# Matmuls without a result at sixteen PE steps of the first two and last two batches of a two-layer cross-attention kernel

## The chip, the cores and the metric

The kernel runs on one core of one Trainium2 chip. The metric is device time in microseconds of one execution. Three runs of the kernel before took 2371.49, 2372.46 and 2372.55 us; the median is 2372.46 us.

## The reference

For each of 64 batches there are 256 positions of 320 channels and a context of 77 tokens of 512 channels. Two cross-attention layers follow each other, each with 20 heads of 16 channels. Layer 0 and layer 1, cut to what is computed:

```python
# layer 0, all tensors per batch and head
q = x @ Wq.T; k = text @ Wk.T; v = text @ Wv.T          # text: the 77 tokens
out = softmax(q @ k.T * D**-0.5) @ v
x = (merge_heads(out) @ Wo.T + bo) + x
# layer 1
text, ip = ctx[:, :-4], ctx[:, -4:]                     # 73 text tokens, 4 image tokens
probs = softmax(q @ k_t.T * D**-0.5)
text_out = probs @ v_t
qsem = l2norm(probs @ text); sem = qsem @ l2norm(ip).T
probs_ip = softmax(q @ k_ip.T * D**-0.5 + 0.5 * sem) * spatial_mask
x = ((text_out + probs_ip @ v_ip) @ W_out + b_out) + x
```

## The kernel before

A first stage (to about 317 us) projects all contexts to keys and values and stores them in HBM. The second stage, `attention`, starts at about 321 us and goes through the 64 batches as a software pipeline. Each step of the pipeline has a name: the layer (0 or 1), a letter and a number. On PE, `q` is the query projection, `s` the scores whose maxima are wanted, `m` the turning of the maxima, `t` the turned scores (of which `0t0`, `0t1`, `0t2` fill PSUM for five exponentials), `a` the product of exponentials and values, `o` the output projection, and in layer 1 `u` and `n` the weighted squares of the semantic part, `i` and `p` the scores and values of the image tokens. ACT takes the exponentials (`ef`), DVE the maxima (`mneg`), the low halves (`q_low`) and the softmax of the image tokens (step `y`, 19 small operations, the last of which writes `pip`), POOL scales by the inverse sums (`ust`) and writes the low half of the attended values (`al`). Inverse sums go through HBM (`rb<-r_dram`), as do the image probabilities (`pt<-p_dram`).

The order on every engine is written out by hand: the table `ORDER` gives a cycle of steps, each with a lag in batches (`0o0/1` is the output projection of layer 0, one batch behind). At the beginning and at the end of the pipeline only the steps whose batch exists stand in the cycle, so PE has fewer of them between two waits. A batch is numbered from 0 to 63.

PSUM has 8 banks. The table `USES` says which steps use which bank, and `Turns` works out who used a bank last. Each PE step begins with `wait_free(...)`, which waits until the last reader of its banks is done, and then waits for its data with `b.reached(...)`:

```python
def turned_scores(l, b, c):
    ...
    wait_free(pe, l, b, *uses)
    if c == 0:
        b.reached(pe, s_ql[l], 2, 1)
        b.reached(pe, s_tw[l], 2, 2)
        b.reached(pe, s_mt[l], 1, 1)
```

For `0t1` the banks' last reader is the exponential of the step before (`0t0`), and there is no wait for data behind it. For the first `0o0` the bank is new and the only wait is for `al`. For the last `1p0` the banks' last readers include step `y` of the same batch, that is `pip`; its data wait is for `pt`, which is `pip` after its way through HBM.

PE's engine runs its instructions in this order, one after the other.

Of the kernel before, what the change touches and what calls it, by code (L numbers as in the profile page):

```python
# [16 lines left out]
B, S, C = 64, 256, 320  # L17
# [80 lines left out]
class Batch:  # L98
# [23 lines left out]
    def reached(self, eng, sem, each, k):  # L122
# [20 lines left out]
        0x/0 1sh/4 1rl/4 1ps/4 1sl/3 0k/0 0ds/1 1v/2 1pl/4 1c/1 0rw/1 0sh/1 0rl/1 1ds/3 1g/1 1ns/3 1d/3 0v/0 1nl/3  # L143
        1rw/3 1vi/2 1st/4 1ss/2 1k/1""",
}

FIRST = {}

# [595 lines left out]
def attention(nc, psum, early, x, k_dram, v_dram, g_dram, c_dram, kip_dram, vip_dram, r_dram, n_dram, s_dram, p_dram,  # L744
# [3 lines left out]
    with ExitStack() as stack:  # L748
# [12 lines left out]
        ident16, sel, pick, kmask, vmask = early.ident16, early.sel, early.pick, early.kmask, early.vmask  # L761
# [66 lines left out]
        def banks(l, use, n=1):  # L828
            r = min(turn_banks.banks(l, use))
            return psum[:, r:r + n, :]  # L830

        def row(l, use, n=1):
            return banks(l, use, n).rearrange("p r n -> p (r n)")
# [4 lines left out]
        def wait_free(eng, l, b, *uses, only=None):  # L838
            turn_banks.wait(eng, freed, b, l, *uses, only=only)

        def keys(l, both_parts, c):

            lead = both_parts * 4 * T + c * 2 * T if c < 2 else 8 * T + both_parts * 2 * T
            return ke[l][:, lead:lead + 2 * T].rearrange("p (e t) -> p e t", e=2)
# [5 lines left out]
        def in_halves(ap, j):  # L850

            return ap.rearrange("p h s -> p (h s)").rearrange("p (z h s) -> p z h s", z=2, s=TS)[:, :, j, :]
# [147 lines left out]
        def _(pe):  # L1000
            def project(o, w, tail, high, low, chunks, packed):

                for at_chunk, c in enumerate(chunks):
                    halves = packed and c == 2
                    cols = slice(c * P, c * P + (HALF if halves else P))
                    parts = [(w[:, hw, k, cols], high, k) for k in (0, 1) for hw in (0, 1)]
                    parts += [(tail[:, cols], high, 2)]
                    parts += [(w[:, 0, k, cols], low, k) for k in (0, 1)]
                    parts += [(tail[:, cols], low, 2)]
                    for n, (a, data, k) in enumerate(parts):  # L1010
                        at_ends = {"start": n == 0, "stop": n == len(parts) - 1}
                        if not halves:
                            mm = pe.matmul(o[:, at_chunk * S:(at_chunk + 1) * S], a, data[:, k, :], **at_ends)  # L1013
                            continue
                        for z in (0, 1):
                            mm = pe.matmul(o[z * HALF:(z + 1) * HALF, 0:TS], a, data[:, k, z * TS:(z + 1) * TS], **at_ends)  # L1016
                return mm

            def query(l, b, n):
                wait_free(pe, l, b, f"q{n}")  # L1020
                b.reached(pe, s_xh[l], 1, 1)
                b.reached(pe, s_xl[l], 1, 1)
                project(row(l, f"q{n}"), wqs[l], wqt[l], xh[l], xl[l], PARTS[n], True).then_inc(f_q[l], 1)

            def scores(l, b, c):

                n = TXT[l]
                uses = [f"s{2 * c}", f"s{2 * c + 1}"]
                wait_free(pe, l, b, *uses)
                if c == 0:  # L1030
                    b.reached(pe, s_qh[l], 2, 1)
                    b.reached(pe, s_ke[l], 16, 16)
                for s in range(2):
                    for j in range(NJ):
                        rows = slice(j * SLOT, (j + 1) * SLOT)
                        o = banks(l, uses[j // 2], 2)[:, j % 2, 0:4 * n].rearrange("p (e s t) -> p e s t", e=2, s=2)
                        mm = pe.matmul(o[:, :, s, :], qh[l][rows, c * S + s * P:c * S + (s + 1) * P],  # L1037
                                       keys(l, 0, c)[rows, :, 0:n], start=True, stop=True)
                if c == 1:
                    b.reached(pe, s_qh[l], 2, 2)  # L1040
                    for j in range(NJ):
                        rows = slice(j * SLOT, (j + 1) * SLOT)
                        o = banks(l, uses[j // 2], 2)[:, j % 2, 4 * n:6 * n].rearrange("p (e t) -> p e t", e=2)
                        mm = pe.matmul(o, qh[l][rows, 2 * S:PW], keys(l, 0, 2)[rows, :, 0:n], start=True, stop=True)
                mm.then_inc(f_s[l], 1)

            def turn_max(l, b, n):
                wait_free(pe, l, b, "m")
                b.reached(pe, s_max[l], MAXIMA, MAXIMA)
                o = row(l, "m").bitcast(F16)  # L1050
                for s in range(2):
                    mm = pe.transpose(o[:, s * P:(s + 1) * P], mneg[l][:, :, :, s].rearrange("p j x -> p (j x)"),  # L1052
                                      ident16[:])
                mm.then_inc(f_m[l], 1)

            def turned_scores(l, b, c):

                n = TXT[l]
                uses = [f"t{2 * c}", f"t{2 * c + 1}"] if c < 2 else ["t4"]
                wait_free(pe, l, b, *uses)  # L1060
                if c == 0:
                    b.reached(pe, s_ql[l], 2, 1)
                    b.reached(pe, s_tw[l], 2, 2)
                    b.reached(pe, s_mt[l], 1, 1)
                if c == 2:
                    b.reached(pe, s_ql[l], 2, 2)
                for e in range(2):
                    if c < 2:
                        tiles = [(slice(j * SLOT, (j + 1) * SLOT),
                                  banks(l, uses[j // 2], 2)[0:n, j % 2, e * S:(e + 1) * S]) for j in range(NJ)]  # L1070
                        cols, many = slice(c * S, (c + 1) * S), S
                    else:
                        tiles = [(slice(j * SLOT, (j + 1) * SLOT), banks(l, "t4", 4)[0:n, j, e * TS:(e + 1) * TS])
                                 for j in range(NJ)]
                        cols, many = slice(2 * S, PW), TS
                    for both_parts, q in ((0, ql[l]), (1, twin[l][:, e, :].bitcast(F16))):
                        for rows, o in tiles:
                            pe.matmul(o, keys(l, both_parts, c)[rows, e, 0:n], q[rows, cols], start=(both_parts == 0),  # L1078
                                      stop=False)
                    for rows, o in tiles:  # L1080
                        k, lead = (2 * c + e, 0) if c < 2 else (2 * c, e * many)
                        mm = pe.matmul(o, sel[rows, k, 0:n], mt[l][rows, lead:lead + many], start=False, stop=True)  # L1082
                mm.then_inc(f_t[l], 1)
# [37 lines left out]
            def square_norms(l, b, k):  # L1121

                if k == 0:
                    wait_free(pe, l, b, "n")
                b.reached(pe, s_wr, UNITS, k + 1)
                pe.wait_ge(s_zero[l], CLEARED[l])
                for j in range(NJ):
                    w = e2[:, k, j, :] if k < UNITS - 1 else in_halves(e2[:, k, :, :], j)
                    mm = pe.matmul(row(l, "n")[j * SLOT:(j + 1) * SLOT, 0:S], pick[:, k, :], w,  # L1129
                                   start=(k == 0), stop=(k == UNITS - 1))  # L1130
                mm.then_inc(f_n, 1)
# [16 lines left out]

            def attend_ip(l, b, n):
                wait_free(pe, l, b, "p")  # L1150
                b.reached(pe, s_vb, 1, 1)
                b.reached(pe, s_pt, 16, 16)
                for c in range(CW):
                    rows = slice(c * SLOT, (c + 1) * SLOT)
                    mm = pe.matmul(banks(l, "p", 3)[:, c, 0:S], vb[rows, :, :].rearrange("p h d -> p (h d)"),
                                   pt[rows, :], start=True, stop=True)
                mm.then_inc(f_p, 1)

            def output(l, b, n):
                wait_free(pe, l, b, f"o{n}")  # L1160
                b.reached(pe, s_al[l], 1, 1)
                project(row(l, f"o{n}"), wos[l], wot[l], ah[l], al[l], PARTS[n], l == 1).then_inc(f_o[l], 1)

            def softmax_turn(l, b, n):
                pass

            program("pe", {"y": softmax_turn, "q": query, "s": scores, "m": turn_max, "t": turned_scores, "a": attend,
                               "u": gram_products, "n": square_norms, "i": ip_scores, "p": attend_ip, "o": output})

        @block.scalar  # L1170
# [425 lines left out]
```

## Time and profile before

| | |
|---|---|
| median of 3 runs | 2372.46 us |
| profiled execution, its own time | 2372.11 us |
| its span (first to last instruction) | 2370.3 us |
| busy share PE, DVE, ACT, POOL | 93%, 78%, 72%, 67% |
| mean granted TensorE clock | 0.984 |

The share of PE is that of the whole span. In the first and the last batches it is lower, and the granted clock, which is 1.0 (2.4 GHz) in most of the span, is 0.5 (1.2 GHz) in stretches there. A line such as `L1078` is the line of the kernel that issued an instruction; `<-ACT ef L1211` behind an idle time says what ended it.

### The profile page before, as it was taken

To read this page: it belongs to the slowest core of one execution; us is meant where nothing else is said; L and a number is where in the kernel's file an instruction comes from. 1 tells how busy PE (TensorE), PEld (TensorE's weight loads), DVE (VectorE), ACT (ScalarE), POOL (GpSimd) and SP (SyncE) were. 2 spreads that over 40 slices of the span, in tenths; PEclk is the share of its full clock that TensorE was granted. 3 is DMA by queue.
4 is the path that set the end of the run, shared out by engine and by line. 5 is a ranking of instruction groups with operands and counts; after the bars stand their busy time and mean duration, and the time that the engine had idled before them with its cause. 6 is when DMAs were issued, how large, how long until landed. Compare 5 with 4: busy or idle time off the path is not lost.

```text
span 2370.3 us, 86625 instructions
## 1 busy us (share of the span) xinstructions
PE 2200.8 (93%) x32824; PEld 1391.7 (59%) x32824; DVE 1849.0 (78%) x3709; ACT 1707.6 (72%) x2732; POOL 1589.4 (67%) x1056
## 2 busy tenths in 40 slices
PE   7999967999999999999999999999999999999984
PEld 5777744555555555555555555555555555555542
DVE  6856644888888888888888888888888888888873
ACT  4323326788888888888888888888888888888862
POOL 4121225777777777777777777777777777777762
PEclk9999988999999999999999999999999999999997
DMA  9877642444444444444444444444444444444431
GB/s 273 267 230 210 204 132 62 114 121 120 123 119 121 117 121 114 117 121 121 122 122 118 120 121 122 120 123 118 122 120 118 114 116 122 123 120 121 118 93 58
DMA packets 338308, 310.64 MB, mean 131 GB/s; under 512 B 180224, under 2 KB 281856, under 8 KB 337920
## 3 DMA queue, kind: packets, MB, share of 16 engines
q1 hardware_dynamic: 337920, 305.36, 46.1%
q8 instruction: 257, 4.21, 0.8%
q14 instruction: 131, 1.07, 0.2%
HBM read 164.66 MB, written 105.98 MB: 114 GB/s over the span
## 4 chain that ended last, share of the span: by engine, by line
PE 44%; POOL 14%; ACT 13%; issue 8%; DVE 3%; DMA 2%; SPq 1%; ACTq 0%; POOLq 0%; DVEq 0%
PE psum L1013 17%; ACT ef L1211 10%; POOL e L1445 7%; PE psum L1117 7%; PE psum L1099 5%; PE psum L1078 5%; POOL ust L1407 5%; PE psum L1016 3%; POOL al L1412 2%; ACT q_high L1192 2%; PE psum L1082 2%; PE psum L1037 2%; PE psum L1129 2%; DMA rb<-r_dram 1%; PE psum L1052 1%
## 5 line engine op out<-in xcount | busy, mean ns | idle before, releaser
L1445 POOL TENSOR_TENSOR e<-ef,eh 73x1024 f32<-73x1024 f32 x320 | 680.3, 2133 | 201.2 <-PE psum L1129 118.5
L1211 ACT ACTIVATE ef<-psum 73x1024 f32<-73x1024 f32 (+1 forms) x640 | 636.2, 1014 | 72.5 <-PE psum L1082 68.6
L1273 DVE TENSOR_REDUCE mneg<-psum 128x8 f16<-128x616 f32 (+3 forms) x512 | 450.9, 934 | 8.9 <-PE psum L1037 2.3
L1301 DVE TENSOR_TENSOR e<-psum,e 73x1024 f32<-73x1024 f32 x320 | 385.6, 1205 | 10.4 <-PE psum L1117 5.8
L1099 PE MATMUL psum<-ef,values 128*32 128x256 f32 x5120 | 360.1, 386 | 0.5
L1117 PE MATMUL psum<-eh,gram 128*73 128x512 f16 x1280 | 337.7, 386 | 18.7 <-DVE mneg L1273 14.2
L1226 ACT ACTIVATE eh<-ef 73x1024 f16<-73x1024 f32 x320 | 337.4, 1055 | 7.7 <-ACT ef L1211 0.4
L1219 ACT ACTIVATE ust<-psum 128x512 f32<-128x512 f32 x384 | 222.4, 596 | 124.0 <-POOL al L1412 116.2
L1407 POOL TENSOR_TENSOR ust<-ust,rb 128x768 f32<-128x768 f32 x128 | 232.3, 1815 | 104.9 <-DMA rb<-r_dram 104.9
L1412 POOL TENSOR_TENSOR al<-ust,ah 128x768 f16<-128x768 f32 x128 | 210.2, 1642 | 85.5 <-ACT ah L1251 85.5
L1281 DVE SCALAR_TENSOR_TENSOR q_low<-psum,q_high 128x512 f16<-128x512 f32 (+1 forms) x256 | 112.8, 481 | 182.4 <-ACT q_high L1192 182.4
L1078 PE MATMUL psum<-q_low,keys 32*73 32x256 f16 (+3 forms) x3072 | 206.7, 265 | 51.5 <-ACT ef L1211 22.5
L1251 ACT ACTIVATE ah<-ust 128x768 f16<-128x768 f32 x128 | 107.9, 843 | 168.0 <-POOL ust L1407 93.0
L1117 PEld LDWEIGHTS psum<-eh,gram 128*73 128x73 f16 x1280 | 120.6, 114 | 158.2 <-DVE mneg L1273 52.6
L1013 PE MATMUL psum<-ah,wo 128*128 128x256 f16 x1280 | 197.2, 278 | 14.7 <-POOL al L1412 14.0
L1078 PE MATMUL psum<-twins,keys 32*73 32x256 f16 (+3 forms) x3072 | 197.3, 251 | 0.0
L1082 PE MATMUL psum<-mt,sel 32*73 32x256 f16 (+3 forms) x3072 | 197.2, 251 | 0.0
L1099 PEld LDWEIGHTS psum<-ef,values 128*32 128x32 f32 x5120 | 134.6, 109 | 101.9 <-issue 31.4
L1078 PEld LDWEIGHTS psum<-q_low,keys 32*73 32x73 f16 (+1 forms) x3072 | 95.5, 109 | 167.1 <-ACT ef L1211 70.3
L1129 PE MATMUL psum<-e,pick 128*32 128x256 f32 x2560 | 166.0, 386 | 5.6 <-DVE e L1301 5.6
L1013 PE MATMUL psum<-xh,wq 128*128 128x256 f16 x1024 | 155.7, 275 | 5.8 <-PEq L244 4.2
L731 POOL TENSOR_TENSOR ch<-cx,one 128x2464 f16<-128x2464 f32 x7 | 30.0, 4292 | 179.0 <-PE psum L449 167.3
(188 smaller groups left out, 4815.0 us busy)
## 6 DMA issues: line engine op xcount, KB each, us to landing
rb<-r_dram SPq DMA_DIRECT2D x128, 384.0 KB, 3.8
keys<-k_dram SPq DMA_DIRECT2D x128, 231.0 KB, 4.0
values<-v_dram SPq DMA_DIRECT2D x128, 192.5 KB
ust<-ust SPq DMA_DIRECT2D x512, 48.0 KB, 2.4
v_dram<-vst SPq DMA_DIRECT2D x64, 320.0 KB
out<-outt SPq DMA_DIRECT2D x64, 320.0 KB, 2.3
k_dram<-kst SPq DMA_DIRECT2D x32, 616.0 KB, 4.0
x<-in_x SPq DMA_DIRECT2D x32, 384.0 KB, 5.1
```

What stands on the lines that cost most here:

```text
L1013: mm = pe.matmul(o[:, at_chunk * S:(at_chunk + 1) * S], a, data[:, k, :], **at_ends)
L1078: pe.matmul(o, keys(l, both_parts, c)[rows, e, 0:n], q[rows, cols], start=(both_parts == 0), stop=False)
L1082: mm = pe.matmul(o, sel[rows, k, 0:n], mt[l][rows, lead:lead + many], start=False, stop=True)
L1099: mm = pe.matmul(row(l, f"a{c}")[j * SLOT:(j + 1) * SLOT, r * S:(r + 1) * S], va[l][:, h, :], e, start=True, stop=True)
L1117: mm = pe.matmul(banks(l, f"u{k}", 2)[0:n, r, :], gm[:, b.parity(), half, :], e, start=(half == 0), stop=(half == 1))
L1211: act.activation(ef[l][0:m, unit_heads(n), :].rearrange("t h s -> t (h s)"), src, ACT.Exp, scale=SM).then_inc(s_exp[l], 1)
L1226: act.activation(eh[0:m, unit_heads(k), :], ef[1][0:m, unit_heads(k), :], ACT.Copy, scale=0.5)\
L1273: dve.tensor_reduce(dst, o, AX_X, ALU.max, negate=True).then_inc(s_max[l], 1)
L1301: dve.tensor_tensor(rest, banks(l, f"u{k}", 2)[0:m, :, :], rest, ALU.mult).then_inc(s_wr, 1)
L1407: pool.tensor_tensor(at(l, b), at(l, b), rb[l][:], ALU.mult).then_inc(s_at[l], 1)
L1412: pool.tensor_tensor(al[l][:], at(l, b), ah[l][:], ALU.subtract).then_inc(s_al[l], 1)
L1445: pool.tensor_tensor(e2[0:m, k, :, :], ef[1][0:m, unit_heads(k), :], eh[0:m, unit_heads(k), :], ALU.subtract).then_inc(s_e2, 1)
```

## The change

A table `IDLE` names sixteen PE steps by name and batch, with a number of matmuls each, 302 in all. A new function `fill_wait`, called in seven of the PE steps right behind `wait_free` and ahead of the waits for data, issues that many matmuls of the 128x128 identity with 128x256 elements of a weight tile. They write the first 256 columns (`S` is 256) of the bank that the step is about to overwrite (`start=True`), so nothing reads their result. No other engine's program is changed.

```diff
+IDLE = {("0q0", 0): 10, ("0s0", 0): 14, ("0s1", 0): 6, ("0m0", 0): 14, ("0t1", 0): 12, ("0t2", 0): 12, ("0s0", 1): 12,
+        ("0s1", 1): 6, ("0m0", 1): 14, ("0o0", 0): 42, ("0t1", 1): 12, ("1m0", 0): 8, ("1n0", B - 1): 22, ("1o0", B - 2): 16,
+        ("1p0", B - 1): 80, ("1o0", B - 1): 22}
...
+            def fill_wait(l, name, n, b, o):
+
+                for _ in range(IDLE.get((f"{l}{name}{n}", b.index()), 0)):
+                    pe.matmul(o[:, 0:S], ident16[:], wqt[0][:, 0:S], start=True, stop=True)
+
             def query(l, b, n):
                 wait_free(pe, l, b, f"q{n}")
+                fill_wait(l, "q", n, b, row(l, f"q{n}"))
                 b.reached(pe, s_xh[l], 1, 1)
...
                 wait_free(pe, l, b, *uses)
+                fill_wait(l, "s", c, b, row(l, uses[0]))
                 if c == 0:
                     b.reached(pe, s_qh[l], 2, 1)
...
                 wait_free(pe, l, b, "m")
+                fill_wait(l, "m", n, b, row(l, "m"))
                 b.reached(pe, s_max[l], MAXIMA, MAXIMA)
...
                 wait_free(pe, l, b, *uses)
+                fill_wait(l, "t", c, b, row(l, uses[0]))
                 if c == 0:
...
                     wait_free(pe, l, b, "n")
+                    fill_wait(l, "n", k, b, row(l, "n"))
                 b.reached(pe, s_wr, UNITS, k + 1)
...
                 wait_free(pe, l, b, "p")
+                fill_wait(l, "p", n, b, row(l, "p"))
                 b.reached(pe, s_vb, 1, 1)
...
                 wait_free(pe, l, b, f"o{n}")
+                fill_wait(l, "o", n, b, row(l, f"o{n}"))
                 b.reached(pe, s_al[l], 1, 1)
```

In the rows below, what stands in brackets are the semaphores for which the instruction waits: `q_low0`, `maxima0`, `exponentials0` count the low halves, maxima and exponentials of layer 0, `ip_probabilities` counts `pip`, `ip_probabilities_loaded` counts `pt`. Line 1026 is `fill_wait`; the lines behind it are thirteen or fourteen higher than before.

PE, batch 0 of layer 0, from the scores `0s0` to the end of `0s1`. Before:

```order
L1037 MATMUL psum<-keys0,q_high0 128x2x77 [waits keys_loaded0,q_high0,q_low0]
L1037 MATMUL psum<-keys0,q_high0 128x2x77 x7
L1037 MATMUL psum<-keys0,q_high0 128x2x77 [waits maxima0]
L1037 MATMUL psum<-keys0,q_high0 128x2x77 x7
L1044 MATMUL psum<-keys0,q_high0 128x154 [waits q_high0]
L1044 MATMUL psum<-keys0,q_high0 128x154 x3
```

Now:

```order
L1026 MATMUL psum<-wqt0,ident16 128x256 [waits q_low0]
L1026 MATMUL psum<-wqt0,ident16 128x256 x13
L1048 MATMUL psum<-keys0,q_high0 128x2x77 [waits keys_loaded0,q_high0]
L1048 MATMUL psum<-keys0,q_high0 128x2x77 x7
L1026 MATMUL psum<-wqt0,ident16 128x256 [waits maxima0]
L1026 MATMUL psum<-wqt0,ident16 128x256 x5
L1048 MATMUL psum<-keys0,q_high0 128x2x77 x8
L1055 MATMUL psum<-keys0,q_high0 128x154 [waits q_high0]
L1055 MATMUL psum<-keys0,q_high0 128x154 x3
```

The wait for `q_low0`, which was one of those of the first score matmul, is now that of the first of the 14 matmuls without a result, and the wait for `maxima0` that of the first of 6. What is left for the score matmuls to wait for are the keys and `q_high0`.

PE, the end of `0t0` and the beginning of `0t1` in batch 0. Before:

```order
L1082 MATMUL psum<-mt0,sel 77x256 x4
L1078 MATMUL psum<-q_low0,keys0 77x256 x4
L1078 MATMUL psum<-twins0,keys0 77x256 x4
L1082 MATMUL psum<-mt0,sel 77x256 x4
L1078 MATMUL psum<-q_low0,keys0 77x256 [waits exponentials0]
L1078 MATMUL psum<-q_low0,keys0 77x256 x3
L1078 MATMUL psum<-twins0,keys0 77x256 x4
```

Now:

```order
L1095 MATMUL psum<-mt0,sel 77x256 x4
L1091 MATMUL psum<-q_low0,keys0 77x256 x4
L1091 MATMUL psum<-twins0,keys0 77x256 x4
L1095 MATMUL psum<-mt0,sel 77x256 x4
L1026 MATMUL psum<-wqt0,ident16 128x256 [waits exponentials0]
L1026 MATMUL psum<-wqt0,ident16 128x256 x11
L1091 MATMUL psum<-q_low0,keys0 77x256 x4
L1091 MATMUL psum<-twins0,keys0 77x256 x4
L1095 MATMUL psum<-mt0,sel 77x256 x4
```

The wait for the exponentials stands ahead of the 12 matmuls, and the turned scores behind them wait for nothing more. `0t1` of batch 1 reads the same; `0t2` of batch 0 has one data wait left behind its fill, for `q_low0`, which counts up long before.

PE, the end of the program: the tail of `1o1` of batch 62 and `1p0` of batch 63. Before:

```order
L1016 MATMUL psum<-ah1,wo1 64x128 [waits attended_low1,ip_attended]
L1016 MATMUL psum<-ah1,wo1 64x128 x7
L1016 MATMUL psum<-ah1,wot1 64x128 x2
L1016 MATMUL psum<-al1,wo1 64x128 x4
L1016 MATMUL psum<-al1,wot1 64x128 x2
L1155 MATMUL psum<-pt,vb 128x256 [waits vip_blocks,ip_probabilities,ip_probabilities_loaded,x_out1,ip_attended]
L1155 MATMUL psum<-pt,vb 128x256 x2
```

Now:

```order
L1020 MATMUL psum<-ah1,wo1 64x128 [waits attended_low1,ip_attended]
L1020 MATMUL psum<-ah1,wo1 64x128 x7
L1020 MATMUL psum<-ah1,wot1 64x128 x2
L1020 MATMUL psum<-al1,wo1 64x128 x4
L1020 MATMUL psum<-al1,wot1 64x128 x2
L1026 MATMUL psum<-wqt0,ident16 128x256 [waits ip_probabilities,x_out1,ip_attended]
L1026 MATMUL psum<-wqt0,ident16 128x256 x79
L1170 MATMUL psum<-pt,vb 128x256 [waits ip_probabilities_loaded,vip_blocks]
L1170 MATMUL psum<-pt,vb 128x256 x2
```

The 80 matmuls wait for `ip_probabilities`; `pt` is waited for behind them.

## Rows read from the trace of the kernel before

**Rows 1.** The page: busy time of each engine; granted TensorE clock in 40 slices.
```profile
PE 2200.8 (93%) x32824; PEld 1391.7 (59%) x32824; DVE 1849.0 (78%) x3709; ACT 1707.6 (72%) x2732; POOL 1589.4 (67%) x1056
...
PEclk9999988999999999999999999999999999999997
```
**Rows 2.** PE in time, from 318 us: start, length, what, [idle before <-what ended it].
```profile
327.64 0.32 PE L1037 MATMUL psum<-keys,q_high 32*128 32x154 f16 x8 [2.28 <-DVE q_low L1281]
328.94 0.32 PE L1037 MATMUL psum<-keys,q_high 32*128 32x154 f16 x8 [0.98 <-DVE mneg L1273]
...
331.70 0.39 PE L1052 MATMUL psum<-ident,mneg 128*128 128x128 f16 x2 [2.35 <-DVE mneg L1273]
...
336.34 0.44 PE L1078 MATMUL psum<-q_low,keys 32*77 32x256 f16 x4 [2.09 <-ACT ef L1211]
...
339.94 0.33 PE L1078 MATMUL psum<-q_low,keys 32*77 32x128 f16 x4 [2.10 <-ACT ef L1211]
...
360.26 1.04 PE L1013 MATMUL psum<-ah,wo 128*128 128x256 f16 x4 [7.10 <-POOL al L1412]
```
**Rows 3.** Chain of waits over the span: start us, length us, what stood on it.
```profile
322.51 4.33 DVE ef L1260
...
340.80 2.92 PE psum L1099 x32
...
360.26 4.26 PE psum L1013 x24
...
391.01 4.16 PE psum L1013 x24
...
422.19 3.93 PE psum L1013 x24
...
454.28 2.62 PE psum L1013 x24
...
2340.13 3.32 PE psum L1013 x16
2353.25 4.31 DMA pt<-p_dram
2362.89 3.58 PE psum L1013 x16
```
**Rows 4.** Windows: busy time of each engine (x instructions), PEclk, DMA share, GB/s.
```profile
325.83:329.10 3.27, 0.48 (x20) 0.29 (x20) 2.77 (x5) 0.00 (x0) 3.27 (x2) 1.00 0.33 109
...
332.70:336.00 3.30, 1.50 (x24) 1.09 (x24) 0.00 (x0) 1.64 (x2) 3.30 (x1) 0.50 0.02 5
...
350.00:360.00 10.00, 0.75 (x14) 0.20 (x6) 3.35 (x7) 1.11 (x2) 3.23 (x2) 0.50 0.54 146
...
363.50:376.90 13.40, 9.40 (x188) 6.08 (x185) 6.33 (x12) 7.81 (x12) 4.87 (x4) 1.00 0.08 20
...
2346.60:2357.60 11.00, 0.00 (x0) 0.00 (x0) 3.96 (x11) 0.36 (x1) 1.80 (x1) 0.50 0.25 67
```
**Rows 5.** PE in time, last 80 us.
```profile
2307.21 1.50 PE L1129 MATMUL psum<-e,pick 128*32 128x256 f32 x24 [0.60 <-DVE e L1301]
2309.90 0.71 PE L1155 MATMUL psum<-pt,vb 32*128 32x256 f32 x6 [1.18 <-ACT ef L1211]
...
2332.22 2.79 PE L1129 MATMUL psum<-e,pick 128*32 128x256 f32 x24 [3.93 <-DVE e L1301]
...
2357.70 1.23 PE L1155 MATMUL psum<-pt,vb 32*128 32x256 f32 x6 [13.70 <-DMA pt<-p_dram]
2362.89 1.01 PE L1013 MATMUL psum<-ah,wo 128*128 128x256 f16 x4 [3.96 <-POOL al L1412]
```
**Rows 6.** DVE in time, last 60 us.
```profile
2344.50 0.22 DVE L1319 TENSOR_SCALAR psum<-n 96x64 int32<-96x64 int32 x1
...
2350.94 0.42 DVE L1358 TENSOR_TENSOR pip<-psum,fm 96x256 f32<-96x256 f32 x1
```
**Rows 7.** DMA issues by SP in time, last 60 us.
```profile
2341.47 0.62 SPq L963 DMA_DIRECT2D n<-n_dram  x1
```

## The prediction

> **What bounds the kernel now.** I read the page first. PE is the busiest engine, 2200.8 us of 2370.3, and its granted clock is full in the middle of the span and lower near both ends [rows 1]. So the change, which touches only the ends, is worth what those ends are worth. Then the chain of waits over the whole span, to see what stands on the path there. In the start it goes through the clearing of `ef` on DVE (4.33 us), the products of batch 0 (2.92 us) and then, once per batch, the output projection of layer 0: the same 24 matmuls take 4.26, 4.16 and 3.93 us the first three times and 2.62 us the fourth [rows 3]. The three long ones are what the low clock costs there: 1.64 + 1.54 + 1.31 = 4.5 us. In the end it goes through the projections of batches 62 and 63 (16 matmuls each, 3.32 and 3.58 us) and the way of `pt` through HBM [rows 3]. At full clock one such matmul takes 2.62 / 24 = 0.109 us, so 16 take 1.75; at half clock I take 0.213 us, which is 256 columns at 1.2 GHz. The windows show where the clock is low: 0.50 from 332.7 to 336.0 with PE busy 1.50 of 3.30 us, 0.50 from 350 to 360 with PE nearly idle, 0.50 from 2346.6 to 2357.6 with PE idle; and 1.00 at 325.8 to 329.1 behind a busy stretch, and from 363.5 to 376.9 [rows 4]. PE in time says what ends its waits there [rows 2, 5].
>
> Whether a fill costs time hangs on which of two waits it stands between. It stands behind the wait for the bank and ahead of the wait for data. Where data come last, the fill runs in the idle time. Where the bank comes last, the idle time stays as it is and the fill follows it. The order of the changed program names the semaphore for which each fill waits, so each of the sixteen places can be sorted.
>
> **The start, part by part.** A delay on the chain of layer 0 reaches the end, because each output projection waits for the one before and PE is full between them.
>
> - `0q0`, 10 matmuls: 1.1 us or a little more, but `q_low` waits for the clearing of `ef`, which ends at 326.84 [rows 3]. Bounds 0 and 0.8; I take 0.
> - `0s0`, 14: the idle 2.28 us is ended by `q_low` [rows 2], and the order shows that this is the bank. All of it is added: 14 x 0.109 = 1.5 (full clock, as [rows 4] show there; 3.0 at half).
> - `0s1`, 6: ended by the first maximum [rows 2], the bank again: 0.65 (1.3 at half).
> - `0m`, 14: nobody has used the bank; 1.5 us fit in the idle 2.35 us [rows 2]. 0; 0.6 if half clock.
> - `0t1` and `0t2` of batch 0, 12 each: both idle times (2.09 and 2.10) are ended by the exponentials [rows 2], the bank. Added: 1.3 each at full clock, 2.6 each at half. The wait of 2.1 us is still there, so I take one of each: 3.9.
> - What a higher clock gives back in these steps: 24 turned scores in 1.50 us at half clock [rows 4] would take 0.75, twice; `0t2` some 0.4; the products of 2.92 us would take 2.0 (24 of the same kind take 1.50 at full clock [rows 5]). At most 0.75 + 0.75 + 0.4 + 0.9 = 2.8; since half the fills were taken at half clock, half of it, -1.4.
> - Batch 1's `0s0`, `0s1`, `0m` (32): off the chain, PE then idles 7.10 us for `al` [rows 2]. They use 18 x 0.109 = 2.0 us of it (the 14 of `0m` go beside DVE). Cost 0 by themselves.
> - `0o0`, 42: new bank, data wait. 4.6 us in the 7.1 - 2.0 = 5.1 left: it just fits at full clock; at half it takes 9.0 and is 3.9 late. I take +0.5 for a part at half clock. The 24 matmuls behind it then run at full clock: -1.6.
> - `0t1` of batch 1, 12: the same wait as above, at full clock, as the window up to 376.9 shows [rows 4]: +1.3.
> - `1m0`, 8: 0.9 us in a data wait. 0.
>
> Sum of the start: 1.5 + 0.65 + 3.9 - 1.4 + 0.5 - 1.6 + 1.3 = +4.8.
>
> **The end.**
>
> - `1n0` of batch 63, 22: the idle 3.93 us is ended by DVE's last `e` [rows 5], which is the bank (`weighted`). PE is at half clock there. How long does it stay so once PE is busy? From the chain: the projection of 4.26 us lost 1.64, so it ran twice that, 3.3 us, at half. With 3.3 us the fill is 15.5 matmuls at half and 6.5 at full clock, 4.0 us. Bounds 2.4 and 4.7. Behind it the 24 and 6 matmul passes (2.79 and 1.23, the latter from the same step at 2357.70) take 1.50 and 0.71 [rows 5]: -1.8. Net +2.2.
> - `1o0` of batch 62, 16: 1.7 us in the wait for `al`. 0, and its 16 matmuls go from 3.32 to 1.75: -1.55. But the softmax of batch 63, which starts at 2344.50 [rows 6], needs two things: the output read and the norms, whose load SP issues only at 2341.47 [rows 7]. The norms path gets all of the +2.2 and nothing back. Their landing isn't shown; it has between no slack and well over 1 us. So this step and the one before make between +0.65 and +2.2 together; I take +1.4.
> - `1p0` of batch 63, 80: the order shows `ip_probabilities`, and `pip` ends at 2351.36 [rows 6]; `pt` lets PE go on at 2357.70 [rows 5]. Room 6.3 us, not the 13.7 of the row. At half clock to begin with [rows 4]: 3.3 us for 15.5, then 64.5 x 0.109 = 7.0, together 10.3. That is 4.0 us too long (2.4 if all at full clock, 10.8 if all at half). Given back: 0.5 in `1p0` and 3.58 - 1.75 = 1.8 in the projection behind it: net +1.6 or 1.7.
> - `1o0` of batch 63, 22: 2.4 us behind DVE's 1 us, within the 3.96 us [rows 5]. 0.
>
> Sum of the end: 1.4 + 1.6 = +3.0. Together +7.8 us on the 2372.11 us of the profiled execution: 2379.9. The median of the runs is 0.35 above it, so 2380.2 us, 0.33% slower.
>
> **The rivals.**
>
> 1. Not slower: the clock stays full wherever fills stand. The rule for it is that a busy PE has the full clock and an idle one loses it; for it, [rows 4] show 1.00 behind busy stretches. Then the start is 1.5 + 0.65 + 2.6 + 1.3 - 2.8 - 1.6 = +1.6, less 2.85 if the second and third projections of [rows 3] are fast too, -1.2; the end is 0.6 (the norms) + 2.4 - 0.5 - 1.8 = +0.7. Total about -0.5: 2372. It decides once both the fills in front of the turned scores and the unfilled projections at 391 and 422 run at full clock. Against it: no fill stands near 391 or 422, and 2.1 us of idle stay in front of each group of turned scores. The Trainium skill's page "TensorE: Matmul & The Clock Gate" says under "Why this matters for your kernels" that TensorE should be kept busy without long gaps to stay at its full rate; by that rule alone this rival's time would come out. The same page says under "What's actually happening" that the rise comes at another point from run to run and is less than 1% of a typical kernel; the first speaks for this rival, the second against building on it. The trace agrees that the stake is small.
> 2. Full clock in the start, but 391 and 422 as before: +1.6 in the start and +3.0 at the end, 4.6: 2377.
> 3. Half clock through most fills of the start: 1.5 + 1.3 + 5.1 + 2.6, and the 42 late by about 3 us, and only 1.6 back: +12 and +3 at the end: 2387. It is spoken for by [rows 4], where 1.50 us of work in 3.30 did not lift the clock.
> 4. The change doesn't do what it says (the bank waits end before the data waits, so that all fills are free): the order excludes it for `0t1`, whose work waits for nothing else.
>
> **How the numbers follow.** Forecast 0.63, rival 1 0.07, rival 2 0.12, rival 3 0.18. About 0.2% or 4.7 us is what a measurement can tell. The forecast's own range is +4.5 to +11, and nearly all of it (0.58) lies over 4.7; with rival 3 slower is 0.77. Rival 2, the foot of the forecast and most of rival 1 make the same 0.20, the rest is faster, 0.03. The range reaches from 2375.0 to 2385.0 and leaves out rival 1 and the upper part of rival 3.
>
> **What would show it.** In the profile of the changed kernel: fills at `0t1` and `0t2` that start when the exponential ends, with the turned scores directly behind them; the first output projection of layer 0 about 4 to 5 us later than 360.26, in 2.6 us; the fill of 80 starting when `pip` ends, not when the projection of batch 62 ends, and still running when `pt` lands; PE busy some 35 to 45 us more. I am wrong if the first projections of [rows 3] are not later than before, or if `pt` lands after the 80.

## The result and the profile after

Six runs of the changed kernel took 2379.90 to 2384.42 us, median 2383.43; six of the kernel before 2371.49 to 2375.35, median 2373.60. The ratio is 1.0039 with a 95% interval from 1.0029 to 1.0049: slower, by 9.8 us in the medians, where 7.8 were forecast. The profiled execution took 2384.42 us with a span of 2382.6, 12.3 us over that of before, which is the longest of its own runs; the terms below come from it.

PE in time, from the changed kernel's trace, at the steps of [rows 2]. L1026 is the fill, L1091 the turned scores, L1017 the projections; the other lines have moved by up to 16 (`mneg` is L1289 for L1273, `ef` L1227 for L1211).

```profile
327.92 1.70 PE L1026 MATMUL psum<-wqt,ident 128*128 128x256 f16 x14 [1.22 <-DVE q_low L1297]
...
330.86 0.83 PE L1026 MATMUL psum<-wqt,ident 128*128 128x256 f16 x6 [0.98 <-DVE mneg L1289]
...
334.32 0.29 PE L1064 MATMUL psum<-ident,mneg 128*128 128x128 f16 x2 [0.69 <-DVE mneg L1289]
...
338.33 2.74 PE L1026 MATMUL psum<-wqt,ident 128*128 128x256 f16 x12 [2.09 <-ACT ef L1227]
341.00 0.44 PE L1091 MATMUL psum<-q_low,keys 32*77 32x256 f16 x4
...
344.31 1.94 PE L1026 MATMUL psum<-wqt,ident 128*128 128x256 f16 x12 [2.10 <-ACT ef L1227]
...
360.84 4.75 PE L1026 MATMUL psum<-wqt,ident 128*128 128x256 f16 x42
366.11 0.61 PE L1017 MATMUL psum<-ah,wo 128*128 128x256 f16 x4 [0.52 <-POOL al L1428]
```

The waits for a bank that [rows 2] showed are still there: 0.98 us for the first maximum, 2.09 and 2.10 for the exponentials. Behind each of them now stands a fill: 6 matmuls (0.83 us), 12 (2.74) and 12 (1.94). The wait for `q_low`, 2.28 us before, is 1.22 us, since the ten matmuls of `0q0` stand ahead of it; its fill of 14 took 1.70 us behind it. The fill of 14 ahead of the turning of the maxima (from 331.93) ran inside its wait, of which 0.69 us are left, and the one of 42 ended in time: 0.52 us were left to wait for `al`.

The chain of waits over the whole span of the changed kernel, the rows that answer to [rows 3]:

```profile
338.33 2.74 PE psum L1026 x12
344.31 1.94 PE psum L1026 x12
347.04 2.69 PE psum L1112 x32
...
366.11 2.79 PE psum L1017 x24
371.78 2.10 PE psum L1026 x12
...
398.34 5.06 PE psum L1017 x24
...
430.04 4.29 PE psum L1017 x24
...
462.48 2.62 PE psum L1017 x24
...
2297.27 2.79 PE psum L1017 x24
...
2339.55 4.88 PE psum L1026 x22
...
2352.28 2.21 DMA n<-n_dram
2361.60 10.96 PE psum L1026 x80
2377.08 1.94 PE psum L1017 x16
```

The fills behind the exponentials are on the chain by name. The first projection of layer 0 starts 5.85 us later than at 360.26 and takes 2.79 us where it took 4.26. Of the 5.85 us 0.29 are not the fills': the clearing of `ef`, with which the chain begins, starts at 322.80 in this trace and at 322.51 in [rows 3]. The fourth projection starts at 462.48, 8.2 us later. From there to the last, at 2297.27 for 2289.21, the lag stays what it is (8.1). At the end the 22 and the 80 are on the chain, and the load of the norms (`n<-n_dram`), which was not on it before.

The clock, in windows of the changed kernel:

```profile
330.00:338.00 8.00, 3.92 (x58) 2.71 (x58) 4.51 (x8) 2.04 (x3) 7.85 (x4) 1.00 0.01 2
338.00:342.00 4.00, 3.67 (x36) 2.53 (x36) 0.00 (x0) 0.27 (x1) 1.10 (x1) 0.57 0.00 0
342.00:345.00 3.00, 0.90 (x15) 0.63 (x8) 0.00 (x0) 1.93 (x2) 0.00 (x0) 1.00 0.00 0
345.20:348.80 3.60, 3.60 (x50) 2.00 (x51) 0.00 (x0) 1.02 (x1) 0.00 (x0) 0.53 0.18 40
349.00:372.00 23.00, 16.69 (x202) 12.74 (x191) 6.92 (x13) 6.66 (x12) 6.45 (x6) 1.00 0.25 69
372.00:375.50 3.50, 3.50 (x38) 2.26 (x36) 0.00 (x0) 0.07 (x1) 2.44 (x3) 0.57 0.00 0
```

PE is busy 3.67 of 4.00 us from 338 to 342 and yet at the lower clock for most of it: the first fill of 12 is paid for at half clock, and the clock rises when it is over. The second (from 344.31) and the third (from 371.78) begin at full clock. The clock falls while they run, and stays low from 345.2 to 348.8 and from 372.0 to 375.5 with PE busy all the time, so that the turned scores and a part of the products or projections behind them pay too.

### The profile page after: what moved, and what is told of

It reads as the page before. It is cut to its first block, busy times and chain, and to the rows that moved or that the text cites. A ratio compares the mean times of both kernels' runs of the same rounds, so it can differ in the third digit from the quotient of the medians.

```text
span 2382.6 us, 87224 instructions
## 1 busy us (share of the span) xinstructions
PE 2234.2 (94%) x33126; PEld 1418.9 (60%) x33126; DVE 1848.8 (78%) x3709; ACT 1707.7 (72%) x2732; POOL 1589.2 (67%) x1056
## 3 DMA queue, kind: packets, MB, share of 16 engines
q8 instruction: 260, 4.26, 0.8%
## 4 chain that ended last, share of the span: by engine, by line
PE 45%; POOL 14%; ACT 13%; issue 8%; DVE 3%; SPq 1%; DMA 1%; ACTq 0%; POOLq 0%; DVEq 0%
PE psum L1017 17%; ACT ef L1227 10%; POOL e L1461 7%; PE psum L1130 7%; PE psum L1112 5%; PE psum L1091 5%; POOL ust L1423 4%; PE psum L1020 3%; POOL al L1428 2%; ACT q_high L1208 2%; PE psum L1095 2%; PE psum L1048 2%; PE psum L1143 1%; PE psum L1064 1%; DVE mneg L1289 1%
## 5 line engine op out<-in xcount | busy, mean ns | idle before, releaser
L1227 ACT ACTIVATE ef<-psum 73x1024 f32<-73x1024 f32 (+1 forms) x640 | 636.2, 1014 | 77.3 <-PE psum L1095 73.4
L1289 DVE TENSOR_REDUCE mneg<-psum 128x8 f16<-128x616 f32 (+3 forms) x512 | 451.0, 934 | 13.2 <-PE psum L1048 5.4
L1317 DVE TENSOR_TENSOR e<-psum,e 73x1024 f32<-73x1024 f32 x320 | 385.3, 1204 | 10.2 <-PE psum L1130 4.6
L1091 PE MATMUL psum<-q_low,keys 32*73 32x256 f16 (+3 forms) x3072 | 206.5, 265 | 45.6 <-ACT ef L1227 16.2
L1017 PE MATMUL psum<-ah,wo 128*128 128x256 f16 x1280 | 195.0, 275 | 2.2 <-POOL al L1428 1.5
L1091 PE MATMUL psum<-twins,keys 32*73 32x256 f16 (+3 forms) x3072 | 196.9, 251 | 0.0
L1091 PEld LDWEIGHTS psum<-q_low,keys 32*73 32x73 f16 (+1 forms) x3072 | 95.4, 109 | 161.2 <-ACT ef L1227 62.9
L1017 PE MATMUL psum<-xh,wq 128*128 128x256 f16 x1024 | 155.7, 275 | 1.6 <-POOL xl L1418 1.4
```

The costliest lines, as they stand in the source:

```text
L1227: act.activation(ef[l][0:m, unit_heads(n), :].rearrange("t h s -> t (h s)"), src, ACT.Exp, scale=SM).then_inc(s_exp[l], 1)
L1289: dve.tensor_reduce(dst, o, AX_X, ALU.max, negate=True).then_inc(s_max[l], 1)
L1317: dve.tensor_tensor(rest, banks(l, f"u{k}", 2)[0:m, :, :], rest, ALU.mult).then_inc(s_wr, 1)
```

## The experiments

Theory A is that of the prediction: a fill costs what of it runs behind the last wait. A fill behind a wait for the bank is all cost, one in a data wait is free as long as it fits. Theory B is that the extra work itself, or where the clock happens to fall, makes the difference. All kernels were timed in rounds with the kernel before; differences are those of the medians.

| kernel | median us | before, same rounds | ratio, 95% interval |
|---|---|---|---|
| e1, first two batches only | 2378.46 | 2373.86 | 1.0022 (1.0013 to 1.0030) |
| e2, last two batches only | 2378.12 | 2373.86 | 1.0018 (1.0009 to 1.0027) |
| e3, data waits only | 2367.68 | 2373.86 | 0.9974 (0.9965 to 0.9984) |
| e4, bank waits only | 2382.73 | 2373.86 | 1.0034 (1.0022 to 1.0047) |
| e5, fills ahead of the bank waits | 2366.20 | 2374.59 | 0.9965 (0.9952 to 0.9979) |
| e6, 30 for 80 | 2377.71 | 2374.59 | 1.0012 (1.0003 to 1.0021) |
| e7, e5 and 28 more | 2361.29 | 2374.59 | 0.9947 (0.9933 to 0.9960) |
| e8, 24 for 12 behind the exponentials | 2386.80 | 2374.59 | 1.0055 (1.0041 to 1.0069) |
| e9, e7 with 120 for 80 | 2362.92 | 2373.14 | 0.9953 (0.9939 to 0.9966) |
| e10, only the exponentials' fills ahead | 2375.51 | 2373.14 | 1.0006 (0.9996 to 1.0015) |

**Start and end apart.** The table `IDLE` cut in two:

```diff
+# e1: only the entries of batches 0 and 1
+# e2: IDLE = {("1n0", B - 1): 22, ("1o0", B - 2): 16, ("1p0", B - 1): 80, ("1o0", B - 1): 22}
```

> Only the twelve fills of the first two batches (186 matmuls). Theory A (a fill behind a bank wait is added to the chain, one in a data wait is free): the start and the end add up. In the two traces the projection of layer 0 in the last batch starts at 2297.27 us with the change and at 2289.21 without, so this kernel is 8.1 us slower than before, 5 to 9 in the median. Theory B (the change mostly displaces where the clock falls, and costs as much as luck has it in projections without a fill): anything from -3 to +5, and the trace shows the difference in the unfilled projections of batches 1 and 2 (1.3 to 2.4 us each), not in front of the turned scores.

> Only the four fills of the last two batches (140 matmuls). Theory A: the span's end is 12.3 - 8.1 = 4.2 us later in the change, all of it in these four: +4.2, 3 to 5, with the 80 matmuls lasting 10 to 11 us and starting when pip ends. Theory B: the clock of the last 40 us is raised by the fills, and what they give back (0.5 + 1.8 + 1.5 + 1.8 us) is more than what they cost: 0 or below.

Measured: +4.6 and +4.3 us. They add up to 8.9, the change has 9.8. (The twelve fills of e1 are 162 matmuls, not 186.) The end is as A said, though the 80 took 11.77 us in e2's trace and not 10 to 11. The start came out just below A's range of 5 to 9 and inside B's of -3 to +5 in the median, and scattered widely, 2373.67 to 2383.88 us in twelve runs. The trace of e1, taken in an execution of 2374.01 us, shows what scatters:

```profile
365.80 2.79 PE psum L1015 x24
...
396.37 3.71 PE psum L1015 x24
...
426.62 2.62 PE psum L1015 x24
...
457.38 2.62 PE psum L1015 x24
```

Here the first projection is 5.5 us late, as in the change (5.85), but the unfilled ones of batches 1 and 2 take 3.71 and 2.62 us where the change's trace has 5.06 and 4.29, and the fourth is only 3.1 us late. So B has a part. Up to 366 us both traces have nearly the same lag, and from there to the fourth projection they part by 4.8 us: 3.0 of them in the two unfilled projections, and 1.6 at `0t1` of batch 1, where the fill and the work behind it ran at full clock in e1 (the fill in 1.48 us for 2.10). Both are places where the clock falls in one run and not in the other. For the first 366 us the verdict is A's.

**Data waits and bank waits apart.**

```diff
+# e3: 0m0 and 0o0 and 1m0 of batches 0 and 1, both 1o0, and ("1p0", B - 1): 30
+# e4: 0q0, 0s0, 0s1, 0t1, 0t2 of batches 0 and 1, and ("1n0", B - 1): 22
```

> Only fills that stand in a wait for data: 0m of batches 0 and 1, the 42, 1m0, the last two 1o0, and 1p0 of the last batch cut from 80 to 30 so that it fits the 6.3 us between pip and pt (30 take 3.3 us for the first 15.5 at half clock and 1.6 for the rest, 4.9). Theory A: nothing is added and the gains stay: 1.6 us for the first projection of layer 0, some 1.5 for the projection of batch 62, 0.5 and 1.8 at batch 63: -2 to -5.5 us, a little faster than before. Theory B: no different from before within 1 us or slower, since the clock falls again somewhere else.

> The complement but for 1p0: only the fills behind a wait for the bank (0q0, 0s0, 0s1, 0t1, 0t2 in batches 0 and 1, and 1n0 of batch 63; 112 matmuls). Theory A: all of it is added and less is given back, since the projections stay at half clock: in the start 1.5 + 0.65 + 3.9 + 1.3 less about 1, in the end 2.2 to 4: +8, 6 to 12, though this kernel has only a third of the change's matmuls. Theory B (cost goes with the number of matmuls or with luck): a third of the change's 10 us, +3 or less.

Measured: -6.2 and +8.9 us. The two parts of one idea have opposite signs, and the 106 matmuls of e4 (the expectation's 112 is a miscount) cost nearly as much as the 302 of the change. This speaks for A and against B in both of its forms. The gain of e3 is a little over A's -2 to -5.5, although not all of its fills fitted: in its trace the 14 of `0m` in batch 0 ran at half clock, stood on the chain with 3.10 us, and `0m` itself came 1.0 us later than in [rows 2]. A data wait is room only for a fill that fits at the clock it meets.

**The same fills on the other side of the wait.** A second table names a bank that is free at that time, and the fill is issued ahead of `wait_free`:

```diff
+AHEAD = {("0s0", 0): 5, ("0s1", 0): 5, ("0t1", 0): 5, ("0t2", 0): 5, ("0s0", 1): 5, ("0s1", 1): 5, ("0t1", 1): 0,
+         ("1n0", B - 1): 4, ("1o0", B - 2): 4, ("1p0", B - 1): 4, ("1o0", B - 1): 4}
...
+                fill_ahead(l, "t", c, b)                    # to psum[:, AHEAD[...], :]
                 wait_free(pe, l, b, *uses)
                 fill_wait(l, "t", c, b, row(l, uses[0]))    # now only where AHEAD has no entry
```

> All 302 fills of the change, with the same numbers at the same steps, but eleven of them (0s0 and 0s1 of batches 0 and 1, 0t1 twice, 0t2, 1n0, both 1o0, 1p0) stand ahead of the wait for the bank and write to another bank that is free at that time. Theory A (the order of wait and fill is the cause): the fills run inside the idle times and the gains of the clock stay: up to 2.8 + 1.6 us in the start, 1.8 + 1.5 + 0.5 + 1.8 = 5.6 in the end; so 5 to 10 us faster than before, and some 16 faster than the change. Theory B (PE's extra work as such, or where the clock falls, costs the time): the same 10 us slower as the change, give or take 3.

Measured: -8.4 us, with the same 302 matmuls with which the change is 9.8 slower. Moving 214 of them makes 18 us. The chain of waits of e5:

```profile
326.96 1.63 PE psum L1027 x14
...
335.52 1.02 ACT ef L1246
336.54 0.04 issue
336.58 0.42 PE psum L1107 x8
...
388.16 4.07 PE psum L1018 x24
...
419.07 3.98 PE psum L1018 x24
```

The turned scores (L1107) now follow the exponential at once, and the fill between them is off the chain. This is the experiment that settles the cause. The moved fills also write to another bank; that this alone matters was not tested apart, but the traces show what the order does: in the change the fill starts when the exponential ends, here it has ended by then. Not every moved fill became free: the 14 of `0s0` are still on the chain, since PE came to them only at 326.96, behind the ten of `0q0` and the query projection.

**Fewer at the end.**

```diff
-        ("1p0", B - 1): 80
+        ("1p0", B - 1): 30
```

> The change with one size other: the fill of the last 1p0 is 30 instead of 80. Theory A: 80 ran 10.96 us where 6.3 to 6.9 are free; 30 take about 4.9 and end before pt lands. The end is 4 us sooner less some loss of clock in the last projection (its 16 matmuls at half clock: up to 1.8): 2 to 4.5 us faster than the change, so +5.5 to +8 against before. Theory B: no difference from the change, +10.

Measured: +3.1 us, 6.7 less than the change; a range of 5.5 to 8 was expected. PE in time at the end of e6:

```profile
2361.09 5.45 PE L1024 MATMUL psum<-wqt,ident 128*128 128x256 f16 x30 [8.29 <-DVE pip L1372]
2366.90 0.71 PE L1168 MATMUL psum<-pt,vb 32*128 32x256 f32 x6 [0.36 <-DMA pt<-p_dram]
```

The 30 took 5.45 us, PE then waited 0.36 us for `pt`, and the projection behind still ran at full clock (16 matmuls in 1.9 us). So 50 matmuls fewer gave back what they cost beyond the room, 10.96 - 5.45 - 0.36 = 5.15 us, and no clock was lost, which the expectation had set off. The other 1.5 us stay unexplained; the scatter of the start is larger than that.

**Filling the gap ahead of the unfilled projections.**

```diff
+IDLE: ("1t2", 0): 14, ("1t2", 1): 14      AHEAD: ("1t2", 0): 6, ("1t2", 1): 6
...
+                if name == "t" and l and r is not None:
+                    pe.wait_ge(s_max[0], MAXIMA * (b.index() + 3))
```

The bank of these two fills has another reader, so they get a wait of their own, for the maxima of layer 0. In e7's trace PE was idle 0.18 us for it in batch 0.

> The kernel with the fills ahead of the bank waits, and 14 more ahead of the last turned scores of layer 1 (1t2) in batches 0 and 1, in the idle time that comes before the unfilled layer-0 projections of batches 1 and 2 (which took 4.16 and 3.93 us in the kernel before, 2.62 at full clock). Theory A: these run at full clock now: up to 1.5 + 1.3 us faster than the kernel without the 28, 8 to 12 faster than before. Theory B: no further gain; the 28 add their 3 us.

Measured: -13.3 us, 4.9 better than e5 in the same rounds. Its chain of waits:

```profile
359.30 2.79 PE psum L1018 x24
...
388.83 2.62 PE psum L1018 x24
...
418.97 2.62 PE psum L1018 x24
...
449.74 2.62 PE psum L1018 x24
```

All projections from the second on take 2.62 us; in e5's trace the second and third took 4.07 and 3.98, so 2.8 of the 4.9 us are theirs; the rest isn't traced. PE in time and the clock around the first exponentials of e7:

```profile
335.44 1.48 PE L1027 MATMUL psum<-wqt,ident 128*128 128x256 f16 x12
337.60 0.31 PE L1109 MATMUL psum<-q_low,keys 32*77 32x256 f16 x4 [0.67 <-ACT ef L1248]
```

```profile
330.00:340.00 10.00, 7.47 (x106) 5.30 (x104) 4.40 (x8) 3.75 (x5) 9.04 (x4) 1.00 0.01 2
340.00:350.00 10.00, 8.68 (x140) 6.06 (x141) 3.17 (x6) 5.17 (x10) 0.00 (x0) 1.00 0.16 38
```

The 12 now start when PE's own work ends, take 1.48 us at full clock, and leave 0.67 of the 2.1 us of idle time. The granted clock is 1.00 throughout 330 to 390 us. Before that it isn't: the ten matmuls of `0q0` took 2.29 us, the 16 matmuls of the query projection behind them 3.36, and `0s0` starts at 329.62, 2.0 us later than in [rows 2], so some of the room in the start was overfilled even here. e7 is the fastest kernel of the study.

**Twice the suspected cost.** `("0t1", 0)`, `("0t2", 0)` and `("0t1", 1)` of the change with 24 instead of 12.

> The change with the three fills behind the exponentials (0t1 and 0t2 of batch 0, 0t1 of batch 1) of 24 instead of 12 matmuls. Theory A: each extra dozen is added: 1.3 us at full clock, 2.6 at half; +3.9 to +6 over the change, less up to 2 if PE is now busy enough to stay at full clock: +12 to +15 against before. Theory B: more filling keeps the clock up and gives back what it costs: +10 or less.

Measured: +12.2 us, 2.4 more than the change; A's range against before was +12 to +15. The trace has the fills at 5.26, 4.46 and 2.79 us on the chain, together 12.5 where the change's had 2.74 + 1.94 + 2.10 = 6.8; some 3 us of that are not in the medians. Theory B's +10 or less is excluded by the median alone: the interval reaches down to 1.0041, which is +9.7 us.

**Only the exponentials' fills moved.** `AHEAD = {("0t1", 0): 5, ("0t2", 0): 5, ("0t1", 1): 0}`, all else as in the change.

> The change with only three of its fills moved: those of 0t1 and 0t2 of batch 0 and of 0t1 of batch 1 (36 of 302 matmuls) stand ahead of the wait for the exponentials and write to a free bank. Theory A, by the terms of the prediction: their cost of 3.9 + 1.3 us goes, and up to 1.4 us more comes back from a higher clock in the turned scores: 5 to 7 us faster than the change, +3 to +5 against before. Theory B (the place of these three makes no difference): +10.

Measured: +2.4 us, 7.4 less than the change (5 to 7 expected, and +3 to +5 against before); the interval includes no difference from before. These 36 of 302 matmuls are the largest part of its loss. The first projection starts at 359.74 us in this trace, 6.4 us sooner than in the change's.

**More at the end.** `("1p0", B - 1): 120` in e7.

> The kernel with the fills ahead of the bank waits and the 28 more at 1t2, with 120 instead of 80 ahead of the last 1p0. In its trace the 80 end 5.21 us before pt lands, the clock falls, the image values take 1.23 us instead of 0.71 and the last 22 take 3.96 us instead of 2.4, which makes the last projection late. Theory A: 120 take 13.1 us and end just before pt: 0.5 + about 1.2 = 1 to 2 us faster than with 80. Theory B: 40 more matmuls cost 4 us or change nothing.

Measured: -10.2 us, where e7 has -13.3; the intervals overlap, and no gain shows. A expected 1 to 2 us. In the trace the 120 did end just before `pt` (PE waited 1.25 us), and the image values took 0.71 instead of 1.23 us. But from the end of `pip` to the end of the last output it is 13.9 us, and 14.1 in e7: `pt` came 0.36 us later by itself, and the projection now waits for `al`. In e7 the slow fill of 22 (3.89 us on its chain) ended at 2355.83, and `al` at 2355.75, so that fill held up nothing worth naming. The expectation took its excess over full clock for a gain; the wait for `al` was right behind it.

## Why the prediction was right

By its own steps, with what the changed kernel's trace and the experiments show:

- **Bank wait or data wait.** Right, and shown by e3 against e4 and by e5.
- **`0q0`**: 0 forecast, with 0.8 as its upper end. In this trace it is 0: the 14 of `0s0` begin 0.28 us later than PE did before, which is the later clearing of `ef`. In the traces of e1, e4 and e6, which have the same ten matmuls, they and the 16 matmuls of the query projection behind them are on the chain (2.29 and 3.20 us in e1), and the 14 begin 0.9 to 1.4 us late. So the upper end was too low.
- **`0s0` and `0s1`**: 1.5 and 0.65 us forecast, 1.70 and 0.83 on the chain. **`0m`**: hidden, as forecast.
- **`0t1` and `0t2` of batch 0**: 3.9 forecast as one fill at each clock; 2.74 + 1.94 = 4.7.
- **Given back there**: 1.4 forecast. The first 24 turned scores got 0.7 us shorter, the second 0.3, the products 0.2 (2.69 for 2.92): 1.2.
- **The 42**: +0.5 forecast, 0 measured; the projection gave back 1.5 (forecast 1.6).
- **`0t1` of batch 1**: 1.3 forecast, at full clock; 2.10. The clock was 0.57 from 372 to 375.5, and the work behind the fill paid as well: 24 turned scores took 1.43 us for 0.83, and 16 matmuls of the query projection 2.16 for 1.85. No term had this.
- **Left out of the sum**: that the second and third projections may get slower. They took 5.06 and 4.29 us for 4.16 and 3.93. In all the lag of this trace is 8.2 us at the fourth projection, against +4.8 forecast; e1's median says +4.6. That the median is so near the forecast is in part luck, since e1's runs scatter over 10 us.
- **`1n0`**: +2.2 forecast from 4.0 us of fill less 1.8. The fill took 4.88 and gave back 1.4: +3.5. Half clock lasted until the fill ended, not the 3.3 us that one projection had shown.
- **The norms**: the step from `1n0` to the softmax was put at +1.4 with 2.2 as its upper end. The chain of the changed kernel, in its last 40 us:

```profile
2346.34 0.67 PE psum L1170 x6
...
2348.93 0.47 ACT nst L1250
2349.41 0.35 SPq L961
...
2351.65 0.54 SPq L934
...
2352.28 2.21 DMA n<-n_dram
...
2354.59 0.23 DVE psum L1335
```

  PE leaves `p` (L1170), and then the norms go through DVE and ACT (`nst`), a store, four other issues of SP and the load: `n` lands at 2354.5 and the softmax begins. The path that the prediction named is the one that decides. The load takes 2.21 us from its issue; from 2341.47 [rows 7] this makes 2343.7 for the kernel before, 0.8 us before 2344.50 [rows 6]. That is the slack that wasn't known. The softmax begins 10.1 us later than before, and the last `e` of DVE, ahead of `1n0`, 7.3 us later. The step came out at the difference, +2.8, over the upper end, since `1n0` was.
- **The 80**: 10.3 us forecast, 10.96 measured; from 2361.60, when `pip` ended, as said. The room was 6.3, so 4.7 were lost (4.0 forecast); 0.5 and 1.6 given back (0.5 and 1.8).
- **`1m0`, the 32 of batch 1 and both `1o0`**: no cost forecast, none seen. PE still waits 0.82 and 0.16 us for `al` behind the fills of the two `1o0`.
- **The signs**: the fills at `0t1` and `0t2` start when the exponential ends, the 80 when `pip` ends, as said. The first projection is 5.85 us later, where 4 to 5 were named, and takes 2.79 us, not 2.6. PE is busy 33.4 us more (2234.2 for 2200.8), where 35 to 45 were named.

So the steps hold, and the sizes are rough. The sum of 7.8 is 2 us short of the medians. By e2, 1.3 of them are the end (+4.3 for +3.0), where the 22 and the 80 ran longer at half clock than was taken. By e1 none are the start, and 0.9 are in neither. In the profiled execution, the longest, the excess is larger and lies mostly in the start: fills at half clock, and the clock in unfilled work, which was in no term. Rival 1, that the clock stays full wherever fills stand, did not come about in the change. It does in the start of e7 from 330 us on, once the fills stand in the idle time and 28 more are added. The rule that the prediction gave for it, a PE kept busy without long gaps, was not enough in the change: no wait of PE between 330 and 345 us is longer than 2.1 us, and the clock fell twice. The page "TensorE: Matmul & The Clock Gate" of the Trainium skill says under "What's actually happening" that the rise comes at another point from run to run; the traces of e1 and the change agree, where the same 12 matmuls of `0t1` in batch 0 took 1.65 and 2.74 us.

## What to carry to other kernels

Before work is put into a wait, ask which semaphore ends that wait and on which side of it the new work stands. Here 302 matmuls cost 9.8 us, and gained 8.4 once 214 of them stood ahead of the wait for the bank and not behind it. It took a second place to write to that was free at the time, and a look at how long the room is when the first of two waits ends (6.3 us, not 13.7).

Filling the idle time of PE to keep its clock up is worth something at the ends of a pipeline: 13.3 us of 2374.6 here, 4.9 of which came with 28 matmuls in one kind of gap. A fill has to fit its wait at the clock that it meets: the 14 of `0m` in e3 took 3.10 us where 2.35 were free.

## What the runs showed of the hardware

Where the clock falls differs from run to run. With the same fills before them, the same two projections took 3.71 and 2.62 us in e1's trace and 5.06 and 4.29 in the change's. The first projection, with the same fills, took 2.79 us in e7's trace and 4.46 in e9's. Five runs each of e5, e7 and e9 lie within 3 to 4 us, and twelve of e1 within 10; but five of e8, whose fills stand behind the waits, lie within 3, so it isn't shown that fills in the idle time narrow the scatter.

The clock can fall while PE is busy. In the changed kernel it was 1.00 from 342 to 345 us, where PE first waited 2.10 us and then began the second fill of 12, and 0.53 from 345.2 to 348.8, with PE busy for 3.60 of 3.60 us. No wait of PE between 330 and 345 us was longer than 2.1 us.

A fill that meets half clock costs up to double: the 22 ahead of `1n0` took 4.88 us where 2.4 is their time at full clock, and the 24 in e8 took 5.26 and 4.46 where 2.6 is.
